# Two low-rank adapted linear layers in one kernel: a first block loaded whole, a bias term moved from the output rows to the rank sums, and a reordered vector queue

## What is computed

```python
def layer_0(x):   # idx0 picks the adapter
    return x @ W0.T + b0 + 2 * (x @ A0[idx0]) @ B0[idx0]
def layer_1(x):   # idx1 picks the adapter
    return x @ W1.T + b1 + (x @ A1[idx1].T) @ B1[idx1].T
x = x + layer_0(x)
x = x + layer_1(x)
```

## Time and profile before

| | |
|---|---|
| median of 3 runs | 311.84 us (310.71 to 312.2) |
| profiled execution, its own time | 312.06 us |
| its span | 310.5 us |
| PE busy | 303.0 us, 98% |
| PE weight loads | 250.1 us, 81% |
| DVE busy | 194.5 us, 63% |
| ACT busy | 90.3 us, 29% |
| POOL busy | 18.6 us, 6% |
| share of the chain that ended last | PE 91%, DVE 4%, ACT 2%, DMA 1% |

### The profile page before, as it was taken

How to read it: one execution, slowest core, us unless ns; L and a number is a source line. 1 busy time by engine, 2 the same in 40 slices (tenths; PEclk the granted TensorE clock), 3 DMA queues, 4 the chain that set the end, 5 groups by cost and what they waited for, 6 DMA issues and landing times.

```text
span 310.5 us, 4006 instructions
## 1 busy us (share of the span) xinstructions
PE 303.0 (98%) x1427; PEld 250.1 (81%) x1427; DVE 194.5 (63%) x328; ACT 90.3 (29%) x144; POOL 18.6 (6%) x43
## 2 busy tenths in 40 slices
PE   6999999999999999998999999999999999999995
PEld 4788898888887488886888888888888888888884
DVE  4777624994749362188897676487486485585312
ACT  4555534012122302293224223232231322232000
POOL 2233240000000010000000000000000000000000
PEclk9999999999999999999999999999999999999999
DMA  6996150000000055504054360440631711602002
GB/s 205 383 372 243 36 183 21 0 0 2 0 0 3 17 179 209 164 1 135 0 193 140 121 179 34 153 146 34 202 128 42 223 62 70 219 36 84 19 34 101
DMA packets 14744, 33.94 MB, mean 109 GB/s; under 512 B 2149, under 2 KB 2277, under 8 KB 14726
## 3 DMA queue, kind: packets, MB, share of 16 engines
q1 hardware_dynamic: 13702, 31.60, 30.0%
q0 software_dynamic: 1024, 2.10, 2.2%
HBM read 22.09 MB, written 11.60 MB: 109 GB/s over the span
## 4 chain that ended last, share of the span: by engine, by line
PE 91%; DVE 4%; ACT 2%; DMA 1%; SPq 0%; issue 0%
PE bank L807 28%; PE bank L921 16%; PE bank L920 16%; PE bank L922 16%; PE bank L940 4%; PE bank L819 3%; PE bank L927 2%; DMA stage<-W 1%; PE bank L895 1%; PE bank L897 1%; PE bank L896 1%; PE bank L821 1%; DVE w L602 1%; PE bank L868 1%; PE bank L906 1%; PE bank L907 1%
## 5 line engine op out<-in xcount | busy, mean ns | idle before, releaser
L807 PE MATMUL bank<-w,w_hi 128*128 128x512 f32 x256 | 80.9, 401 | 0.8 <-ACT w L350 0.6
L807 PEld LDWEIGHTS bank<-w,w_hi 128*128 128x128 f32 x256 | 49.2, 194 | 13.1 <-ACT w L350 1.3
L807 PE MATMUL bank<-w,w_lo 128*128 128x512 f32 x128 | 49.0, 390 | 0.0
L407 ACT CAST xa<-xr 128x512 fp32r<-128x512 f32 x32 | 19.6, 621 | 33.6 <-PE bank L927 17.3
L807 PEld LDWEIGHTS bank<-w,w_lo 128*128 128x128 f32 x128 | 24.1, 188 | 5.1
L921 PE MATMUL bank<-w_lo,w 128*128 128x512 f32 x64 | 25.1, 392 | 0.0
L922 PE MATMUL bank<-w_hi,w 128*128 128x512 f32 x64 | 25.1, 392 | 0.0
L920 PE MATMUL bank<-w_hi,w 128*128 128x512 f32 x64 | 25.0, 391 | 0.0
L921 PE MATMUL bank<-w 128*128 128x512 f32 x64 | 25.0, 391 | 0.0
L920 PE MATMUL bank<-w 128*128 128x512 f32 x64 | 25.0, 391 | 0.0
L920 PE MATMUL bank<-w_hi,xa 128*128 128x512 f32 x64 | 25.0, 390 | 0.0
(11 more groups left out here) (127 smaller groups left out, 493.4 us busy)
## 6 DMA issues: line engine op xcount, KB each, us to landing
xr<-xT SPq DMA_DIRECT2D x32, 256.0 KB, 4.2
out<-stage SPq DMA_DIRECT2D x28, 256.0 KB, 2.0
stage<-W SPq DMA_DIRECT2D x7, 512.0 KB, 5.0
stage<-W1T SPq DMA_DIRECT2D x7, 512.0 KB, 5.9
a<-rb_rows SPq DMA_DIRECT2D x8, 392.0 KB
rb_rows<-a SPq DMA_DIRECT2D x3, 512.0 KB
rb_rows<-b0w SPq DMA_DIRECT2D x3, 512.0 KB
out<-rows SPq DMA_DIRECT2D x4, 256.0 KB, 2.7
```

What stands on the lines that cost most here:

```text
L407: nc.scalar.copy(x_op(j, 0), raw(j)).then_inc(op_hi[j], 1)
L807: return mm(d_bank(m, h)[:, :], left[:, m, k * P:(k + 1) * P], right[:, k, h * HALF:(h + 1) * HALF], start=start, stop=stop)
```

## The change

- `WARM` is 13 and not 7.
- Block 0 of W0 and of W1ᵀ is loaded as one transfer each. ScalarE copies block 0 of W0 whole, then the second half of W1ᵀ (the half without a diagonal), then the first. The low parts come as W0, second half, first half. TensorE takes the products of block 0 in that order: high·high of half 1, of half 0, then W0's low part, then W1ᵀ's low halves. `splits(k)` is 2k + 3. The two index transfers and the one of b0 are issued behind block 0 and not behind block 1.
- `t_blk` and its products go. `t_sum` is written to DRAM (`t_dram`) and read back as `t_cols`, rows 16 to 31 by batch row (rows 0 to 15 are zero); `stack_h` adds `t_cols[:, b]` while it adds up the rank sums. Both DMAs are on SP's queue behind `load_x(0)`.
- On VectorE the wait for `bounced` and the memsets of ones stand ahead of `low_top(3)`, and `stack_h(0)` ahead of the low parts of S2 and T2.
- Tensors are allocated in another order: `idx`, `ones_b` and `b0_raw` first; `b0w` is 288 words wide for each k and not 258.

The core of the diff:

```diff
-WARM = 7
+WARM = 13
+        idx = sb("idx", [1, 2 * B], I32)
+        ones_b = sb("ones_b", [P, B], F32)
+        b0_raw = sb("b0_raw", [P, KT], F32)
         w0_hi = sb("w0_hi", [P, KT, D], F32R)
...
-        b0w = sb("b0w", [P, KT, 2 * BR + 2], F32R)
+        b0w = sb("b0w", [P, KT, 2 * BR + 32], F32R)
+        t_cols = sb("t_cols", [2 * RK, B], F32)
+        t_sum = sb("t_sum", [P, 1], F32)
...
+        t_dram = nc.dram_tensor("t_sums", (BR, 1), F32, kind="Internal").ap()
...
 # sync: loads
-                if k > 0:
-                    sp.dma_start(stage_w(k, 0), W0[k * P:(k + 1) * P, :]).then_inc(w0_landed[s], DMA)
-                    sp.dma_start(stage_w(k, 1), W1T[k * P:(k + 1) * P, :]).then_inc(w1_landed[s], DMA)
-                else:
-                    for n, (which, a, b) in enumerate(FIRST):
-                        sp.dma_start(stage_w(0, which)[:, a:b], (W0, W1T)[which][0:P, a:b]).then_inc(first_landed[n], DMA)
-                if k == 1:
+                sp.dma_start(stage_w(k, 0), W0[k * P:(k + 1) * P, :]).then_inc(w0_landed[s], DMA)
+                sp.dma_start(stage_w(k, 1), W1T[k * P:(k + 1) * P, :]).then_inc(w1_landed[s], DMA)
+                if k == 0:
...
             sp.wait_ge(lora_lo, 3)
             load_x(0)
+            sp.wait_ge(aux_done, AUX_ST + 1)
+            sp.dma_start(t_dram, t_sum[:, :]).then_inc(t_bounced, DMA)
+            sp.wait_ge(t_zeroed, 1)
+            sp.wait_ge(t_bounced, DMA)
+            sp.dma_start(t_cols[RK:2 * RK, :], t_dram.rearrange("(b r) o -> r (b o)", r=RK),
+                         allow_slow_non_contiguous=True).then_inc(t_landed, DMA)
...
 # scalar: high_w
                 act.wait_ge(diag_added, 2 * k + 1)
                 nc.scalar.copy(w0_hi[:, :, k * P:(k + 1) * P],
                                stage_w(k, 0).rearrange("p (m c) -> p m c", m=KT)).then_inc(hi_made, 1)
+                if k == 0:
+                    act.wait_ge(w1_landed[0], DMA)
+                    nc.scalar.copy(w1_hi[:, 0, HALF:D], stage_w(0, 1)[:, HALF:D]).then_inc(hi_made, 1)
+                    act.wait_ge(diag_added, 2)
+                    nc.scalar.copy(w1_hi[:, 0, 0:HALF], stage_w(0, 1)[:, 0:HALF]).then_inc(hi_made, 1)
+                    return
...
 # vector: low_w
+                if k == 0:
+                    for n, h in enumerate((1, 0)):
+                        cols = slice(h * HALF, (h + 1) * HALF)
+                        dve.wait_ge(hi_made, n + 2)
+                        nc.vector.tensor_tensor(w1_lo[:, 0, cols], stage_w(0, 1)[:, cols], w1_hi[:, 0, cols], ALU.subtract
+                                                ).then_inc(lo_made, 1)
+                    return
...
 # vector: stack_h
-                nc.vector.tensor_tensor(h_sum[:, :], bank[0:2 * RK, 0:T], h_tmp, ALU.add).then_inc(h_added, 1)
+                if b == 0:
+                    dve.wait_ge(t_landed, DMA)
+                nc.vector.scalar_tensor_tensor(out=h_sum[:, :], in0=bank[0:2 * RK, 0:T], scalar=t_cols[:, b:b + 1],
+                                               in1=h_tmp, op0=ALU.add, op1=ALU.add).then_inc(h_added, 1)
...
+            nc.vector.memset(t_cols[:, :], 0.0).then_inc(t_zeroed, 1)
...
-            dve.wait_ge(aux_done, AUX_ST + 1)
-            nc.vector.tensor_scalar(t_blk[:, :], same_batch[:, :, 0], t_sum[:, 0:1], None, ALU.mult
-                                    ).then_inc(st_step, 1)
...
             sum_s4(0)
+            dve.wait_ge(bounced, 8 * DMA)
+            for s in range(2):
+                nc.vector.memset(h_stack[s][6 * RK:6 * RK + 2, :].bitcast(F32), 1.0).then_inc(ones_set, 1)
             low_top(3)
             low_x(S1, 0)
             low_x(S4, 0)
             low_bottom(7)
+            stack_h(0)
             low_x(S2, 0)
             low_t(0, T2)
-            dve.wait_ge(bounced, 8 * DMA)
-            for s in range(2):
-                nc.vector.memset(h_stack[s][6 * RK:6 * RK + 2, :].bitcast(F32), 1.0).then_inc(ones_set, 1)
-            stack_h(0)
...
 # tensor: block 0
+            for n, h in enumerate((1, 0)):
+                pe.wait_ge(hi_made, n + 2)
+                for m in TILES[:FIRST_M]:
+                    d_pass(m, h, 0, w0_hi, w1_hi, True, False)
+            pe.wait_ge(lo_made, 1)
+            for h in (1, 0):
+                for m in TILES[:FIRST_M]:
+                    d_pass(m, h, 0, w0_lo, w1_hi, False, False)
+            for n, h in enumerate((1, 0)):
+                pe.wait_ge(lo_made, n + 2)
+                for m in TILES[:FIRST_M]:
+                    d_pass(m, h, 0, w0_hi, w1_lo, False, False)
...
-                mm(bank[0:B, :], ones_b[:, :], bias_sum[:, cols], start=True, stop=False)
-                mm(bank[0:B, :], t_blk[:, :], b1_raw[:, cols], start=False, stop=True).then_inc(c_summed, 1)
+                mm(bank[0:B, :], ones_b[:, :], bias_sum[:, cols], start=True, stop=True).then_inc(c_summed, 1)
```

More of the change, by code:

```diff
@@ L69, in lora_pair @@
         h_sum = sb("h_sum", [2 * RK, T], F32)
-        t_blk = sb("t_blk", [P, B], F32)
         ident = sb("ident", [P, P], F32)
         same_batch = sb("same_batch", [P, B, RK], F32)
[L73 to L76, removed]
         rb_dram = nc.dram_tensor("rb_rows", (B, STACK, D), F32, kind="Internal").ap()
+        t_dram = nc.dram_tensor("t_sums", (BR, 1), F32, kind="Internal").ap()
         bias_sum = rows[:, 0:2, :].rearrange("p a n -> p (a n)")
@@ L132, in lora_pair @@
         w0_landed = [sem(f"w0_landed{s}") for s in range(STAGE_SLOTS)]
-        first_landed = [sem(f"first_landed{n}") for n in range(4)]
         warm_set = sem("warm_set")
@@ L166, in lora_pair @@
         aux_done = sem("aux_done")
+        t_zeroed = sem("t_zeroed")
+        t_bounced = sem("t_bounced")
+        t_landed = sem("t_landed")
         bias_step = sem("bias_step")
@@ L197, in slot_uses @@
         def slot_uses(k):
-            return k // STAGE_SLOTS + (k % STAGE_SLOTS > 0)
+            return k // STAGE_SLOTS + 1
         def splits(k):
[L203 to L214, removed]
+            return 2 * k + 3
         def stage_w(k, which):
@@ L343, in high_w @@
             def high_w(k):
[L344 to L351, removed]
                 act.wait_ge(diag_added, 2 * k + 1)
@@ L495, in low_w @@
             def low_w(k):
[L496 to L506, removed]
                 for which, landed in ((0, w0_landed), (1, w1_landed)):
                     dve.wait_ge(landed[k % STAGE_SLOTS], slot_uses(k) * DMA)
+                    if k == 0 and which == 0:
+                        dve.wait_ge(ident_made, 2)
                     block_k = stage_w(k, which)[:, k * P:(k + 1) * P]
                     nc.vector.tensor_tensor(block_k, block_k, ident[:, :], ALU.add).then_inc(diag_added, 1)
-                dve.wait_ge(hi_made, splits(k - 1) + 1)
+                dve.wait_ge(hi_made, splits(k - 1) + 1 if k else 1)
                 nc.vector.tensor_tensor(w0_lo[:, :, k * P:(k + 1) * P],
@@ L835, in _ @@
                 mm(banks[7][:, :], xa[:, 0, 0, 0:P], xa[:, 0, 0, :], start=True, stop=True)
-            for n, (ms, h) in enumerate(((TILES[0:3:2], 0), (TILES[0:3:2], 1), (TILES[1:2], 0), (TILES[1:2], 1))):
-                pe.wait_ge(hi_made, min(n + 2, 4))
-                for m in ms:
+            for n, h in enumerate((1, 0)):
+                pe.wait_ge(hi_made, n + 2)
+                for m in TILES[:FIRST_M]:
                     d_pass(m, h, 0, w0_hi, w1_hi, True, False)
-            for h in range(NH):
-                pe.wait_ge(lo_made, h + 1)
+            pe.wait_ge(lo_made, 1)
[4 more added lines that the diff above has]
+                pe.wait_ge(lo_made, n + 2)
                 for m in TILES[:FIRST_M]:
                     d_pass(m, h, 0, w0_hi, w1_lo, False, False)
[L845 to L849, removed]
             for k in range(1, KT):
@@ L867, in _ @@
                 for n in range(2):
-                    last = mm(banks[6 + AUX_ST % 2][:, 0:2 * BR + 2], a1[:, k, n * BR:(n + 1) * BR], b0w[:, k, :],
+                    last = mm(banks[6 + AUX_ST % 2][:, 0:2 * BR + 2], a1[:, k, n * BR:(n + 1) * BR], b0w[:, k, 0:2 * BR + 2],
                               start=(k == 0 and n == 0), stop=(k == KT - 1 and n == 1))
@@ L886, in _ @@
             pe.wait_ge(t4_made, 2)
-            pe.wait_ge(st_step, 3)
+            pe.wait_ge(st_step, 2)
             pe.wait_ge(b1_landed, B * DMA)
```

## The result

The changed kernel takes 307.32 us (median of 4 runs, 306.86 to 307.65) against 311.64 in the same measurement; the ratio is 0.9863, with a 95% interval of 0.9834 to 0.9892. The profiled execution took 307.65 us with a span of 306.1, 4.4 less than before. The forecast was 307.4.

A forecast was written before the change was run, and what follows sets the result against it. TensorE, busy in 98% of the span, was taken as the bound. Savings of 1.2 + 1.7 + 1.35 + 0.3 = 4.55 us gave 307.5 from the profiled 312.06, 307.3 from the median; predicted 307.4, range 306.2 to 309.2.

The forecast's parts named there:

- The first block: Start of the kernel: two whole transfers and 13 zeros bring block 1's first product from 12.7 to 11.5, saving 1.2 us.
- my bound of 5.7: Block 0's load: earliest landing of the second transfer, 0.92 MB at 405 GB/s after 128 KB at 3.46; 6.4 was taken.
- my best case of 11.3: Start of the kernel: second transfer lands at 5.7, block 0 runs at full speed until 11.3, saving 1.4 us.
- Its reason for the high level: Block 0's products: 5.5 us of gapless work ahead, more than preceded the rise at 11.33, so 2.4 GHz was assumed.
- Bias sums: Adapter two: t_blk's products with B1 go, purely TensorE's time, saving 1.7 us; the way through DRAM stays hidden.
- The price of the longer add: stack_h on VectorE: the add with two sums in one instruction, taken at nothing because hidden under other engines' work.
- Rank rows first: Ahead of the first rank product: moving stack_h(0) ahead of S2's and T2's low parts closes a 1.35 us gap.
- The moved wait: VectorE ahead of low_top(3): the wait for eight rank-row transfers costs nothing, with 0.2 us of margin at p1(0).
- Rival A: The moved wait shows: transfers 5% longer make a 0.8 us gap ahead of p1(0), 308.2 us; chance 0.14.
- Operand places: r's sums and the aux product: new tensor places speed the products, between nothing and 0.57 us, 0.3 taken.
- The sum, 4.55: Whole kernel: savings of 1.2, 1.7, 1.35 and 0.3 us, taken from the profiled 312.06 us.
- Rival B: Start of the kernel: the clock stays low through block 0, total saving only 2.75 us, 309.2 us; chance 0.08.

The follow-up runs named there:

- experiment 9: Changed kernel with one more 512 KB transfer ahead of the eight carrying the rank rows, the wait for all nine ahead of low_top(3): one run, 307.48 us.
- experiment 4: The changed kernel itself, measured once more: 307.43 us, ratio 0.9833.
- experiment 6: Kernel before with only the bias sums of adapter two moved (t_blk's products out, t_sum through DRAM): 310.13 us, ratio 0.9942.
- experiments 1 to 4: Kernel before with 13 zeros, 0.9984; changed kernel with 7 zeros, 0.9906; changed kernel with block 0 in four pieces, 0.9857; changed kernel again, 0.9833.
- Experiment 5: Kernel before with only VectorE's order changed (wait, memsets of ones and stack_h(0) moved as in the change): 310.23 us, ratio 0.9963.
- experiment 10: Changed kernel with the extra 512 KB transfer, the wait and memsets between low_top(3) and S1's low part: one run, 307.89 us.
- 11: Changed kernel with 11 zeros, the wait and memsets behind low_bottom(7), directly ahead of stack_h(0): 307.18 us, ratio 0.9822.
- experiments 4 and 7: The changed kernel measured again, 307.43 us; and the changed kernel with tensors in the old order and b0w 258 words wide, 307.25 us.

## Why the prediction was right

**The first block: right in size, with a wrong input, and so close by luck.** 1.2 us forecast, 1.22 found. The landing was mis-sized: 5.5 instead of 6.4, below my bound of 5.7. The bound took the first 128 KB at 3.46 as given and the rest at 405 GB/s; but the pieces were slow from the start (281 GB/s from 3.0 to 5.5 us, the whole transfers 392). The estimate by the Trainium skill ("DMA: Bandwidth & Descriptors", section on the anatomy of one DMA), 5.4, which I had set aside for the rows of the pieces, was nearer. In this execution the error cost nothing, because zeros held TensorE until 7.39. Where the pace rose during the zeros, it counts: in experiment 9 the first real product started at 6.27, behind the copy of the early half, and block 1 at 10.5, beyond my best case of 11.3.

The two profiled executions differ by what was forecast, but single ones spread more widely than that. Block 1 began at 11.9, 12.7 and 13.9 in the three traces with pieces and 7 zeros, and at 10.5 to 11.7 in the six with whole transfers and 13 zeros: 1.8 us apart in the mean. The rest of the change is worth 3.2 us (240.51 less 237.32), so by the medians the first block brought 1.1 us in the measurement of the result (311.64 to 307.32) and 2.0 in that of experiment 4 (312.61 to 307.43). The forecast rests on one trace of the kernel before, and its text gave no warning of this. Its reason for the high level, that more work without a gap goes ahead than in the trace of the kernel before, doesn't settle it: in experiment 6 seven zeros were enough, in three other traces they were not. What holds is that all eight traces with 13 zeros are at the faster pace by the second or third real product.

As experiments 1 to 4 show, neither part has the gain alone. More zeros without the whole block gave 0.5 us, within an interval that takes in nothing. The whole block with 7 zeros has a ratio of 0.9906 where the changed kernel has 0.9863 and 0.9833, so it is 1.3 to 2.3 us slower. With the zeros in place the whole block is worth 0.8. Which part of it does this, the longer rows, the smaller number of transfers or the new order of copies and products, was not tested apart.

**Bias sums: right.** 1.72 us, all of it TensorE's; the way through DRAM stayed hidden, though the 128 words alone took 6.9 us to be written (below). The price of the longer add, taken at nothing, is 0.06 to 0.09 us and hidden only because stack_h(0) was moved too.

**Rank rows first: right.** 1.32 us against 1.35, and 0.1 from the product behind. Experiment 5 has it alone.

**The moved wait: right, margin and all.** 0.24 us of margin against 0.2, of which TensorE's start 0.10 us behind the low part (experiment 9) takes a part. Experiment 9 shows that the margin is real (transfers 0.6 us later, p1(0) 0.45 us later), 10 that another place in the same queue has no such edge, 11 that the third place costs 0.6. Rival A is therefore the true weakness, though it didn't come true.

**Operand places: this step failed.** "If that is the cause, 48 × 0.0054 = 0.26 us go", and 0.31 more at the aux product: 0.3 taken, 0.06 found, and 0.02 between experiments 4 and 7. In the changed kernel r's products stand as before, 22 steps in 5.10 us:

```profile
97.75 0.39 PE L888 MATMUL bank<-w,b0w 128*128 128x512 f32 x1
...
102.85 0.40 PE L889 MATMUL bank<-w,b0w 128*128 128x512 f32 x1
```

and the aux product takes 2.19 us against 2.20, by the chain of waits:

```profile
46.30 2.19 PE bank L860 x16
```

The Trainium skill ("TensorE: Matmul & The Clock Gate", section on LDWEIGHTS) prices a weight load by its columns alone; the runs agree (237.34 us with the old places, 237.32 with the new). Why r's products take 0.232 us each and a D tile's 0.227, at equal columns, stays open. The sum, 4.55, was 0.15 us more than the 4.40 that the two spans differ by. That 307.4 met the median within 0.1 is partly luck: the changed kernel's median lay 0.33 below its profiled execution.

**Rival B, the low clock, didn't come true.** In eight profiles with 13 zeros the first real product came at 6.27 to 7.41, and the pace was 0.23 us from the second or third product on.

## What to carry to other kernels

A gain at the very start of a kernel should be read from several profiles: landings and the clock's rise moved by 1 to 3 us from run to run, more than the effect, while everything behind them repeats within 0.05 us. Filler work pays when it fills the whole wait and the work behind it can then run without a gap, so it belongs together with transfers that land at a steady time. When a wait is moved up in an in-order queue, list every consumer behind it with its due time: one place had 0.24 us of margin, another cost 0.6 us, and the free one was where the engine had been idle anyway.

## What was not expected of the hardware

- With block 0 as two transfers of 4 KB rows the queues moved 387 GB/s from 3 to 7 us (338 to 387 in nine traces), as four with rows of 1 to 3 KB 274 (255 to 307 in five); and the pieces' landings spread over 1.6 us, the whole ones' over 0.25.
- A write of 128 single words from 128 partitions to DRAM took from 49.32 to 56.19 us, 6.9 us from its issue (7.2 to 8.3 in ten other traces), though all queues together moved 1 GB/s in that time:

```profile
49.32 0.33 SPq L261 DMA_DIRECT2D t_sums<-t_sum  x1
56.19 0.33 SPq L264 DMA_DIRECT2D t_cols<-t_sums  x1
```

- A ninth transfer of 512 KB ahead of eight, which had taken 20.7 us together, lengthened them by 0.6 us only.
- With the same 13 zeros from 1.69 on, the pace of 2.4 GHz came at times that differ by about 3 us between executions: starts 0.43 us apart end at 4.4 in experiment 9 and at 7.8, behind the first real product, in experiment 10. Thirteen zeros at 1.2 GHz end at 7.41, since the first step is 0.59 us and not 0.43; the prediction had 7.25.
- The level can be reached and lost again within a few us: experiment 6 has products near the 2.4 GHz pace from 6.90, at 1.2 GHz from 9.11 and at 2.4 GHz again from 12.3, with 1.85 and 0.95 us without work in between.
